# Projection stage of a graph-attention + mixture-of-experts layer: LayerNorm statistics spread over the nodes' evacuations, accumulators cleared on GpSimd, a shorter fill of the score buffer

## What is computed

```python
xn = layernorm(x)                       # mean and variance per node
q, k, v, skip = xn@Wq+bq, xn@Wk+bk, xn@Wv+bv, xn@Ws+bs
e = (edge_attr @ We)                    # per edge
alpha = sum(q[dst] * (k[src] + e)) / sqrt(32)   # per edge and head
alpha = softmax of alpha over the edges of one dst
out = segment_sum((v[src] + e) * alpha, dst) + skip
x = x + out
x = x + moe_ffn(layernorm(x))           # top-2 of 8 experts
```

## Time and profile before

| what | value |
|---|---|
| median of the runs | 2624.8 us |
| profiled execution, first to last instruction | 2619.3 us |
| TensorE busy | 2428.7 us (93%) |
| VectorE busy | 2026.0 us (77%) |
| GpSimd busy | 1856.0 us (71%) |
| ScalarE busy | 1595.0 us (61%) |
| mean granted TensorE clock | 0.96 |

### The profile page before, as it was taken

One profiled execution on the slowest core, in us unless ns is written; L12 is line 12 of the kernel. 1 busy time (PEld: TensorE's weight loads), 2 busy tenths in 40 slices (PEclk: granted clock), 3 DMA queues, 4 the chain that ended last, 5 costly groups with the idle time before them and its releaser, 6 DMA issues. The chain is left out here.

```text
span 2619.3 us, 69697 instructions
## 1 busy us (share of the span) xinstructions
PE 2428.7 (93%) x14190; PEld 1970.3 (75%) x14191; DVE 2026.0 (77%) x5205; ACT 1595.0 (61%) x4422; POOL 1856.0 (71%) x2184
## 2 busy tenths in 40 slices
PE   5997899999999999999999999999996456999998
PEld 2443688888888888888888888887884455999998
DVE  5765899999999999999999999998996774222222
ACT  1222477667667767777767767776775124666665
POOL 5233588888888888888888888888885303666666
PEclk9998999999999999999999999999999557999999
DMA  7323677777787777777777777777772672443443
GB/s 219 113 98 119 208 226 225 221 226 223 221 226 227 222 224 223 222 222 226 223 223 225 225 223 224 227 227 217 225 225 84 198 206 51 71 65 62 70 67 54
DMA packets 337703, 476.84 MB, mean 182 GB/s; under 512 B 61318, under 2 KB 268492, under 8 KB 337052
## 3 DMA queue, kind: packets, MB, share of 16 engines
q0 software_dynamic: 92576, 259.72, 38.5%
q1 hardware_dynamic: 238492, 213.23, 26.7%
q10 hardware_dynamic: 6288, 0.05, 0.1%
HBM read 425.40 MB, written 50.57 MB: 182 GB/s over the span
## 5 line engine op out<-in xcount | busy, mean ns | idle before, releaser
L762 POOL DMA_INDIRECT kv_ring<-vk_table,tab_c x880 | 864.6, 983 | 294.6 <-issue 227.4
L917 PE MATMUL ps_e<-we_sb,aT 128*128 128x256 f32 x3520 | 914.6, 382 | 14.5 <-DVE ve_ke L1008 12.5
L1002 DVE TENSOR_TENSOR ve_ke<-kv_ring,ps_e 128x512 f32<-128x512 f32 x880 | 601.2, 683 | 81.4 <-issue 34.7
L917 PEld LDWEIGHTS ps_e<-we_sb,aT 128*128 128x128 f32 x3520 | 602.1, 191 | 69.4 <-issue 15.9
L772 POOL TENSOR_TENSOR w_ring<-ve_ke,ea 128x264 f32<-128x264 f32 x880 | 567.8, 648 | 22.4 <-PE ps_u L969 6.4
L969 PE MATMUL ps_u<-w_ring,sel 128*128 128x264 f32 x1760 | 541.4, 389 | 10.6 <-DVE acc L1068 4.3
L850 ACT COPY aT<-ps_t 128x256 f32<-128x256 f32 x880 | 326.3, 371 | 347.2 <-PE ps_t L905 215.0
L921 PE MATMUL ps_e<-q_parts,selT 128*128 x2640 | 433.2, 273 | 0.0
L1068 DVE TENSOR_TENSOR acc<-acc,ps_u 128x264 f32 x880 | 369.2, 420 | 24.4 <-issue 9.0
L989 DVE TENSOR_REDUCE alpha<-ve_ke 128x8 f32<-128x256 f32 x880 | 365.5, 415 | 5.8 <-issue 3.5
L1008 DVE TENSOR_TENSOR ve_ke<-ve_ke,ps_e 128x256 f32<-128x256 f32 x880 | 361.2, 410 | 1.9
(11 more groups left out here) (247 smaller groups left out, 2695.6 us busy)
## 6 DMA issues: line engine op xcount, KB each, us to landing
a_ring<-in_edge_attr SPq DMA_DIRECT2D x880, 128.0 KB
loc_c<-loc_table SPq DMA_DIRECT2D x220, 128.0 KB
kv_ring<-vk_table,tab_c POOLq DMA_INDIRECT x880
vk_table<-kv_out SPq DMA_DIRECT2D x49, 256.0 KB
skip_table<-skip_out SPq DMA_DIRECT2D x49, 128.0 KB
q_parts<-skip_table SPq DMA_DIRECT2D x7, 896.0 KB, 10.7
xn_table<-acc SPq DMA_DIRECT2D x7, 896.0 KB, 7.5
out<-q_parts SPq DMA_DIRECT2D x1, 6144.0 KB
```

The costliest lines, as they stand in the source:

```text
L762: g.indirect_dma_start(out=kv_ring[:, i % N_KV, :], out_offset=None, in_=vk_table, in_offset=bass.IndirectOffsetOnAxis(ap=tab_c[:, c % N_T ...
L917: t.matmul(ps_e[i % 2][:, 0:D], aT[i % 2][:, k * P:(k + 1) * P], we_sb[:, k, :], start=(k == 0), stop=(k == KD - 1))
L1002: v.tensor_tensor(both, kv.rearrange("p (t h c) -> p t h c", t=2, c=C), by_head(e, C)[:, None, :, :].to_broadcast([P, 2, H, C]), ALU.add). ...
```

## The change

In the projection block:

- `measure(g)` and `refine(g)` are cut into single instructions and placed between the four instructions of `evacuate`: tiles 0 to 3 of a group carry the `bn_stats` and `bn_aggr` of the next group (two tiles' worth each, one in the fourth, which also adds epsilon), tile 4 the five steps of `refine`. The waits are on counters of their own.
- `normalise` moves from in front of `evacuate` to behind it, for tile j + 3, with three `xn` buffers (NXN = 3).
- `floats`, `locals_` and `masks` are cut into steps, one per tile, behind `normalise`; `columns` starts at tile 8 instead of 6, `masks` at 16 instead of 14. TensorE's index transposes and SP's table stores move with them.
- GpSimd clears `acc` tile by tile (`clear`, L350 of the new file), 50 fills of 128 x 264, each once the x tiles under it have been read.

In the score block VectorE no longer clears `acc`, and sets in `ve_ke` only the count columns of the 32 message slots.

```diff
-            xn = [sb1(f"xn{i}", [P, D]) for i in range(2)]
+            NXN = 3
+            xn = [sb1(f"xn{i}", [P, D]) for i in range(NXN)]
...
-            FLOATS, LOCALS, TURNS, MASKS = 2, 4, 6, 6 + IB + 1
-            RUNS_OUT, LOCS_OUT, TAB_OUT = 4, 7, MASKS + 2
+            FLOATS, LOCALS, TURNS, MASKS = 2, 4, 8, 8 + IB + 1
+            RUNS_OUT, LOCS_OUT, TAB_OUT = 4, 9, MASKS + 4
...
+                def last_x_under(k):
+                    return min(NT - 1, ((k + 1) * UW - 1) // D)
+
+                def clear(k):
+                    pool.wait_ge(s["skip_out_ready"], at("skip_out_ready", last_x_under(k)))
+                    g.memset(acc[:, k, :], 0.0).then_inc(s["acc_cleared"], 1)
...
+                    while cleared < NT + 1 and last_x_under(cleared) < j:
+                        clear(cleared)
+                        cleared += 1
+                pool.wait_ge(s["acc_cleared"], NT + 1)
...
-                    dve.wait_ge(s["xn_turned"], at("xn_turned", j - 2))
-                    v.tensor_scalar(xn[j % 2][:, :], x_sb[:, j, :], mv[:, j, 0:1], rstd[:, j:j + 1],
+                    if j % SG == 0:
+                        dve.wait_ge(s["refined"], at("refined", j // SG))
+                    dve.wait_ge(s["xn_turned"], at("xn_turned", j - NXN))
+                    v.tensor_scalar(xn[j % NXN][:, :], x_sb[:, j, :], mv[:, j, 0:1], rstd[:, j:j + 1],
...
-                def evacuate(j):
+                def evacuate(j, between):
...
+                    between(0)
...
+                AHEAD = 2
+                REFINED_IN = (SG + 1) // 2
+
+                def statistics(j, place):
+                    g, r = j // SG + 1, j % SG
+                    if g >= NGR:
+                        return
+                    first = g * SG
+                    if r < REFINED_IN:
+                        tiles = [t for t in (2 * r, 2 * r + 1) if t < SG]
+                        if place < 2 and place < len(tiles):
+                            measure(first + tiles[place])
+                        elif place == 2:
+                            for t in tiles:
+                                aggregate(first + t)
+                        elif place == 3 and r == REFINED_IN - 1:
+                            variance(g)
+                    elif r == REFINED_IN:
+                        refine(g, place)
+                        if place == 3:
+                            refine(g, 4)
...
                 for j in range(NT):
-                    if j + 2 < NT:
-                        normalise(j + 2)
-                    evacuate(j)
-                    if j % SG == 1 and j // SG + 1 < NGR:
-                        measure(j // SG + 1)
-                    if j % SG == 4 and j // SG + 1 < NGR:
-                        refine(j // SG + 1)
+                    evacuate(j, lambda place: statistics(j, place))
+                    if j + AHEAD + 1 < NT:
+                        normalise(j + AHEAD + 1)
+                    if 0 <= j - FLOATS < 2:
+                        floats(j - FLOATS)
...
-                v.memset(acc[:, :, :], 0.0).then_inc(s["setup"], 1)
-                v.memset(ve_ke[:, :, :], 1.0).then_inc(s["setup"], 1)
+                v.memset(by_head(flat(ve_ke[:, 0:2 * CH, :]), CP)[:, :, C:CP], 1.0).then_inc(s["setup"], 1)
```

More of the change, by code:

```diff
@@ L493, in _, with floats, locals_ @@
                 then(v.memset(q_parts[:, :, NT, :], 0.0))
[L495 to L509, removed]
+                def floats(step):
+                    if step == 0:
+                        dve.wait_ge(gathered[0], 16 * IB)
+                        v.tensor_scalar(run_f, run_g[:, :, :], BIG, None, ALU.mult).then_inc(tables_ready, 1)
+                    else:
+                        dve.wait_ge(gathered[1], 16 * IB)
+                        v.tensor_copy(src_f, src_g[:, :, :])
+                def locals_(step):
+                    if step == 0:
+                        dve.wait_ge(gathered[2], 16 * IB)
+                        then(v.tensor_copy(loc_f, sel_g[:, :, :]))
+                    elif step == 1:
+                        for b in range(IB):
+                            last = v.tensor_scalar(loc_f[:, b, :], loc_f[:, b, :], nt_back[:, b:b + 1], -1.0, ALU.add, ALU.max)
+                        then(last)
+                    elif step == 2:
+                        then(v.tensor_scalar(loc_f, loc_f, float(P), None, ALU.min))
+                        dve.sem_inc(tables_ready, 1)
+                    else:
+                        v.tensor_copy(loc_b[:, :, :], loc_f).then_inc(tables_ready, 1)
                 def columns(b):
@@ L519, in columns @@
                     v.tensor_copy(dst_loc[:, some, :], m[:, 3 * P:3 * P + n].rearrange("p (c i) -> p c i", i=CH)).then_inc(turned_copied, 1)
[L521 to L533, removed]
@@ new lines, in measure, with aggregate @@
+                def measure(j):
+                    for i, (ga, gb) in enumerate(pieces):
+                        if j == ga * SG:
+                            dve.wait_ge(x_loaded[i], 16 * (2 if i == len(pieces) - 1 else 1))
+                    v.bn_stats(stat[:, j, :], x_sb[:, j, :]).then_inc(s["stat_ready"], 1)
+                def aggregate(j):
+                    dve.wait_ge(s["stat_ready"], at("stat_ready", j))
+                    v.bn_aggr(mv[:, j, :], stat[:, j, :]).then_inc(s["aggregated"], 1)
@@ L577, in _ @@
+                for j in range(SG):
+                    measure(j)
+                for j in range(SG):
+                    aggregate(j)
+                variance(0)
+                for step in range(REFINEMENTS):
+                    refine(0, step)
+                for j in range(AHEAD + 1):
+                    normalise(j)
                 dve.wait_ge(w_loaded, 16 * 8)
+                assert REFINED_IN + AHEAD + 1 <= SG
                 for j in range(NT):
-                    if j + 2 < NT:
-                        normalise(j + 2)
@@ L984, in _ @@
                 v.memset(key_prev[:, :], -BIG).then_inc(s["setup"], 1)
[L985 removed]
+                dve.wait_ge(s["setup"], 6)
                 def reduce(c, par, i):
```

76 lines of the change are left out of this document (47 added, 29 removed).

## The result

The changed kernel takes 2596.3 us (median of 4 runs, 2595.2 to 2597.1), the kernel before beside it 2624.5 us (4 runs, 2622.6 to 2625.5): a ratio of 0.9888 with a 95% interval of 0.9876 to 0.99, 28.2 us faster. Forecast were 2598 us and 26.4 us. The profiled executions differ by less, 2619.3 - 2595.3 = 24.0 us, and it is these that the terms are read from. Two words for what follows: a *stall* is idle time of TensorE in front of `turn`, and a *cold* `project` is one that runs at the lower level of TensorE's granted clock (1.2 in place of 2.4 GHz) for part of its time.

A forecast was written before the change was run, and what follows sets the result against it. TensorE's projection block held 24.9 us excess, mostly waiting for VectorE's late xn; the score block waited for VectorE's fills. 24.9 - 3.7 - 0.6 - 2.5 = 18.1, + 9.5 - 1.2 = 26.4; 2624.8 - 26.4 = 2598 us, range 2590 to 2609.

The forecast's parts named there:

- Score start: Start of the score block: VectorE's first add waits for TensorE's edge tile at 258.45 instead of coming at 267.34; 9.5 us gained.
- Tail: End of the projection block: four GpSimd fills of 0.3 us stand behind its last split; 1.2 us lost (0.6 to 2).
- Statistics, whole stalls gone: Projection block: with statistics in pieces xn is done about 2.9 us after the evacuation's start; stalls of four tiles in seven go.
- Normalise three ahead, three buffers: Projection block: xn keeps the same place in VectorE's order, and the third buffer only removes an already satisfied wait; worth 0.
- The third evacuation: Projection block: the unexplained late evacuation at 45.61 us comes again and keeps a 3.7 us stall (0 to 6.0).
- refine, 2.5 us: Projection block: last two refine steps and xn wait beside GpSimd's q splits; 2.5 us of stall stay over six groups (0 to 4.2).
- masks, 0.6 us: Projection block: three tiles where a 1.06 us masks step stands beside two small ones run 0.2 us over; 0.6 us (0 to 2).
- The sum's base: Whole kernel: the runs' median lies 5.5 us above the profiled span, kept when turning the 26.4 us gain into 2598 us.
- Rival B: Projection block: GpSimd's splits hold VectorE's statistics, epsilon and xn in 24 tiles, 9.6 us more stay; 2608 us, chance 0.15.
- Rival C: Score block starts no sooner than its loads (gathers, edge features); only 3 of 9.5 us come; 2604.5 us, chance 0.10.
- D: Projection block: GpSimd becomes the bound through slow fills; a 3.1 us fill gives 2648 us, 23 us slower; chance 0.03.

## Why the prediction was right

The time and the range held: 26.4 us forecast, 28.2 (interval some 26 to 33) measured. The main mechanisms held too; that the number came so near is in part luck, since misses in several terms cancel. By its own steps:

- **Score start, 9.5 us**: right in size (8.3 + 1.3 = 9.6), and the bound was the one named, TensorE's first edge tile. The sum inside was another: the 8.8 us up to that tile came, the clock's part did not last, and 0.8 us came because the first edge tile was done 16.2 us behind the end of GpSimd's work instead of 17.0. The prediction also did not ask what each fill costs alone: either would have been hidden behind the wait for that tile.
- **Tail, 1.2 us**: 1.3 measured, a fill 0.32.
- **Statistics, whole stalls gone**: they went, by the mechanism forecast; the pieces fit ahead of xn, and it ends 2.8 us after the first evacuation's start against 2.9. What the prediction did not see is that the cutting was not needed for them: a whole lump one place later, behind xn, does as well.
- **Normalise three ahead, three buffers, 0**: the third buffer is worth nothing, and xn keeps its place among the evacuations. But with the same move floats, locals and masks came to stand behind an xn instead of between an evacuation and the next xn; that the prediction did not weigh, and how much of their gain it is and how much the cutting was not separated in full.
- **The third evacuation, 3.7 us kept**: a late evacuation came again, the second now, and cost 6.2 us, just above the 6.0 given as its end (5.9 to 9.2 in the runs). The load of x is not its cause; the row of index gathers is. This term is mis-sized by 2.5 us.
- **refine, 2.5 us**: the waiting behind GpSimd is real, 0.22 us in a late group, 1.45 once, beside the resets, which the prediction had overlooked: 1.7 in all, 0.8 less than taken.
- **masks, 0.6 us**: no stall. With the 0.8 us that I could not assign, the block's gain comes out 1.9 us under the forecast (2.5 - 0.8 - 0.6 + 0.8).
- **The sum's base**: I kept 5.5 us between span and time. The run whose profile is shown has 2597.1 - 2595.3 = 1.8. The profiled execution of before was thus likely one of the quicker, and the 24.0 us between the spans understate the gain: 16.2 + 8.3 = 24.5 us in the trace, 26.4 forecast, 28.2 between the medians. The trace is the stricter test, and by it the forecast was 1.9 us too high; the nearer match with the medians comes from no term.

Rival B (splits bind VectorE) happens in the refine tile but costs little there. The longest that one of VectorE's operations took beside GpSimd is the add of 2.81 us, and there it was `resets`, not a split. The Trainium skill, "SBUF — State Buffer", section "Who interferes with whom", names two SBUF inputs and a GpSimd instruction that reads SBUF as what contends. The traces agree: the 2.81, 1.38 and 0.68 us rows are all operations with two SBUF inputs beside a GpSimd subtraction, and the same operations take 0.41 and 0.16 us elsewhere. One-input operations were held too: xn for 0.97 us beside a split, and the fourth step of `refine` for 0.85 until a fill's end. Rival C did not come: TensorE waits for edge features about as long behind the last `project` as before (237.22 - 221.36 = 15.9 us, 15.2 before), and the whole 8.3 us came nonetheless. D fell with the fill's 0.32 us.

## What to carry to other kernels

On an engine that feeds another and has slack, a long piece of work can be cut up ahead of the result that the other waits for, or put whole behind it; the second needs slack enough until the next result but one. Here a lump of 3.1 us fitted two tiles' 3.3 us, lumps of 4.4 and 4.6 us, each one tile behind another, did not. Before charging a removed fill in full, ask what else the first user waits for: two fills can each be free and only together cost. And when small VectorE operations look slow, look at what GpSimd does at that moment, and try moving that.

## What the runs showed of the hardware beyond this

While GpSimd issued its row of index gathers, VectorE and ScalarE acted on some of TensorE's finished matmuls 4 to 8 us late, on others at once; why is open. The second evacuation stood at 43.24 us with the `project` ended at 37.74, at 45.66 in the run with two buffers, at 42.23 with the load of x taken away, and at 38.05 and 38.33 in the two runs where the last seven gathers came later; in the kernel before it stood at 37.77, on time, and the third was the late one. And an operation of VectorE can last longer than the GpSimd instruction beside it: 2.81 us for an add of otherwise 0.41, beside a subtraction of 1.68 us. A gather's issue ran in its first 0.55 us; whether that held it too the trace does not show.
